# One closing unit for each tile of the shared expert, and the small transfers of the softmax shifts issued by ScalarE

## The chip, the cores and the metric

The kernel runs on one core of a Trainium2 chip. The metric is the time of one execution on the device in microseconds (us), as the median of several runs; less is better. TensorE is called PE here, VectorE DVE, ScalarE ACT, GpSimd POOL and SyncE SP; SP does nothing but issue transfers and wait. A transfer that an engine issues goes into a queue of that engine, and all queues share the core's 16 DMA engines.

## The reference

One post-norm transformer layer over 8 batches of 512 tokens, 256 wide, in float32:

```python
x = layernorm(x + attention(x, w_qkv, w_out))          # 16 heads of 16, causal
x = layernorm(x + ffn(x))
# ffn: softmax router over 16 experts, the 6 highest of probs + gate_b are taken,
#   y = sum over them of prob * (silu(x W1' + b1) * (x W3' + b3)) W2' + b2     (176 hidden)
#   z = (silu(x ws1' + bs1) * (x ws3' + bs3)) ws2' + bs2                       (352 hidden)
#   ffn(x) = y + z
```

## The kernel before

The engines run programs of their own, written out by hand, and meet at semaphores. There are four stages.

**Attention.** A loop over 8 batches `b`, in each four groups `g` of four heads, in each eight substeps `s`; the order of each engine's work in a substep is fixed by tables (`PE_ORDER`, `MISC`, `FILLS_OF_SUB`, `SHIFT_AT`). Group number G is 4b + g. PE computes the scores twice: once two groups ahead to find each row's maximum (line 722 and the causal mask of line 724; DVE reduces them, line 1347), and once transposed (line 737) for the exponential on ACT (line 1059), 12 fills to a group. For the second, the negative maximum is part of the operand: `stack_q` has 96 rows with three bfloat16 parts of q and below them 3 rows, the *shift*, with three bfloat16 parts of the maxima. PE transposes the maxima of the next group (stage `m`, line 769), ACT copies them out, DVE splits them in three (`split_shift`, lines 1405 to 1411), and three transfers of 4 KB each carry them into the rows (`load_shift`, line 537). At the start of a group PE waits for the stack and for the shift:

```python
pe.wait_ge(stack_loaded, 192 * (b + 1))
pe.wait_ge(shift_loaded, 48 * (G + 1))
```

In group 0 of a batch PE also projects q, k and v of the next batch. ACT and POOL split them, and SP issues twelve transfers of 256 KB into the other copy of the stacks (`load_stack`, line 531, six for q and six for k). PE needs all twelve at substep 0 of group 2, where it begins to look for maxima in the next batch's scores. Other stages of the batch before ride along: `t0`, `t1` transpose its attention output (PE line 781, in substep 7 of group 0 and substep 1 of group 1; ACT copies them), `p0`, `p1` project it, `x0`, `x1` transpose the normalized result (group 2), `r`, `d` route and rank. POOL scatters the rows to the experts' regions in DRAM.

In the kernel before SP issues the shift of a group as soon as DVE has split it. In its program it stands between the stack's transfers, the load of the residual and the stores of the normalized rows.

**Shared expert, first part.** 10 of 16 chunks of 256 tokens, three tiles to a chunk, 30 tiles `T`.

**Experts.** 208 blocks of 128 rows; POOL adds each block's result to `x1_d` or `z_d` in DRAM with an accumulating transfer.

**Shared expert, second part, and the closing pass.** Tiles T = 30 to 47. For each tile PE multiplies up (`shared_up`, line 707), ACT applies silu (line 1208), DVE multiplies (`hide`, line 1663), ACT rounds (`high`), `low` takes the remainder (on DVE line 1669, on POOL line 1890), and PE multiplies down (`shared_down`, line 930) two tiles later. The closing pass has 16 units `m` of 256 tokens: SP loads both halves of a unit (`load_final`, line 642), POOL adds them (`final_sum`, line 1927), DVE adds the shared expert's result for the six late chunks and takes mean and variance (`final_stats`, lines 1715 to 1727), POOL raises the variance to the power -0.5 (`final_inverse`, line 1940), DVE forms -mean/std (`final_shift`, line 1733), ACT normalizes (`normalized`, line 1264, two instructions to a unit), SP stores. Before, a unit goes in with every second tile from T = 35 on, so that 7 units have their statistics begun in the tiles and 9 behind them; `low` is DVE's for T below 34 and POOL's from 34 on, and for each unit DVE waits for POOL's inverse straight behind the statistics of the next.

Of the kernel before, what the change touches and what calls it, by code (L numbers as in the profile page):

```python
# [30 lines left out]
GH = 4  # L31
NG = HEADS // GH
SUBS = 8
STACK = 6 * HD
SHIFT_ROWS = 3
# [16 lines left out]
HALF = 2  # L52
# [55 lines left out]

SPLIT_X_AT, LOW_X_AT = (3, 1), (3, 3)
# [49 lines left out]
FINAL_ORDER = (10, 0, 11, 1, 12, 2, 13, 3, 14, 4, 15, 5, 6, 7, 8, 9)  # L159
FINAL_FROM = T1 + 5  # L160
DVE_LOW_AFTER = 4
# [5 lines left out]


def final_of(T):

    return (T - FINAL_FROM) // 2 if T >= FINAL_FROM and (T - FINAL_FROM) % 2 == 0 else None


FINAL_IN_TILES = len([T for T in range(T_SH) if final_of(T) is not None])


# [48 lines left out]
def postln_layer(nc, xT, x, wqk, wv, wo, gw, gb, ws, we, b13, b2s, out):  # L225
# [17 lines left out]
    with ctx:  # L243
# [274 lines left out]
        def _(sp):  # L518
# [14 lines left out]
            def load_shift(G, par, gpar, g):  # L533

                sp.wait_ge(shift_step, 3 * G + 3)
                for j in range(SHIFT_ROWS):
                    sp.dma_start(
                        stack_q[par][STACK + j:STACK + j + 1, GH * g:GH * g + GH, :], shift_parts[gpar][j][:]
                    ).then_inc(shift_loaded, 16)

            def iteration(b, par):
# [8 lines left out]
                load_shift(4 * b + 1, par, 1, 1)  # L550
# [6 lines left out]
                load_shift(4 * b + 2, par, 0, 2)  # L557
# [6 lines left out]
                load_shift(4 * b + 3, par, 1, 3)  # L564
# [5 lines left out]
                if not last:  # L570
                    load_shift(4 * b + 4, 1 - par, 0, 0)
# [94 lines left out]
            load_shift(0, 0, 0, 0)  # L666
# [381 lines left out]
        def _(act):  # L1048
# [211 lines left out]
            def normalized(m):  # L1260
                i = FINAL_ORDER[m]
                act.wait_ge(fin_shift_done, m + 1)
                for q in range(HALF):
                    last = nc.scalar.activation(fin_x[i][:, q, :], fin_x[i][:, q, :], ACT.Identity,
                                                bias=fin_shift[:, i, q:q + 1], scale=fin_rstd[:, i, q:q + 1])
                last.then_inc(fin_done, 1)
# [62 lines left out]
        def _(dve):  # L1329
# [380 lines left out]
            def final_stats(m):  # L1710
# [7 lines left out]
                for q in range(HALF):  # L1718
                    last = nc.vector.bn_stats(fin_stats[:, i, q, :], fin_x[i][:, q, :])
# [3 lines left out]
                for q in range(HALF):  # L1723
                    last = nc.vector.bn_aggr(fin_mv[:, i, q, :], fin_stats[:, i, q, :])
                last.then_inc(fin_mv_done, 1)
                dve.wait_ge(fin_mv_done, m + 1)
                nc.vector.tensor_scalar(fin_var[:, i, :], fin_mv[:, i, :, 1], EPS, None, ALU.add).then_inc(
                    fin_var_done, 1)

            def final_shift(m):  # L1730
                i = FINAL_ORDER[m]
                dve.wait_ge(fin_rstd_done, m + 1)
                nc.vector.scalar_tensor_tensor(fin_shift[:, i, :], fin_mv[:, i, :, 0], -1.0, fin_rstd[:, i, :], ALU.mult,
                                               ALU.mult).then_inc(fin_shift_done, 1)
# [32 lines left out]
            for m in range(FINAL_IN_TILES, HALVES):  # L1767
                final_stats(m)
                final_shift(m - 1)
            final_shift(HALVES - 1)  # L1770


        @block.gpsimd
        def _(pool):
# [162 lines left out]
            def final_inverse(m):  # L1937
                i = FINAL_ORDER[m]
                pool.wait_ge(fin_var_done, m + 1)
                nc.gpsimd.tensor_tensor(fin_rstd[:, i, :], fin_var[:, i, :], half_neg[:, 0:HALF], ALU.pow).then_inc(  # L1940
                    fin_rstd_done, 1)

            for T in range(T1 + DVE_LOW_AFTER, T_SH):
                m = final_of(T)
# [3 lines left out]
                if m:  # L1948
                    final_inverse(m - 1)
                low(T)  # L1950
                if m is not None:
                    final_sum(m + 2)
            for m in range(FINAL_IN_TILES, HALVES):
                final_inverse(m - 1)
                if m + 2 < HALVES:
                    final_sum(m + 2)
            final_inverse(HALVES - 1)
# [66 lines left out]
```

## Time and profile before

| | us |
|---|---|
| median of 3 runs (lowest to highest) | 1195.66 (1192.45 to 1196.21) |
| the profiled execution, its own time | 1196.26 |
| its span from first to last instruction | 1194.3 |
| attention, about 30 to 518 of the span | 488 |
| shared expert, first part, and tables, 518 to 620 | 102 |
| experts, 620 to 1120 | 500 |
| second part and closing pass, 1120 to the end | 74 |

Over the whole span PE is busy for 1059.2 us (89%), DVE 745.7 (62%), ACT 666.2 (56%), POOL 750.0 (63%). The profiled execution took 0.6 us more than the median, 1.96 us of its time lie outside its span. In the rows below a line such as `[2.71 <-DMA stack_q<-shift_l]` says that the engine sat idle for 2.71 us ahead of this instruction and what ended the wait.

### The profile page before, as it was taken

The page shows a single profiled execution, that of the slowest core. Times are in us where ns is not written, and L with a number is a line of the kernel's source. Part 1 is how long each engine was busy: PE and PEld are TensorE (multiplying, and loading weights), DVE is VectorE, ACT ScalarE, POOL GpSimd, SP SyncE. Part 2 cuts the span into 40 slices and gives each one's busy share as a digit, 9 for nine tenths or more (in the row PEclk, how much of TensorE's full clock was granted, in tenths as well). Part 3 has the DMA queues.
Part 4 walks back from the last instruction along what each step waited for, and adds up shares of the span by engine and source line. Part 5 has one row for each costly group of instructions (what it writes and reads, how often), then busy time and mean ns, then how long its engine had stood idle before and what let it go on. Part 6 is the DMA issues. An engine that isn't in the chain of part 4 may idle for free.

```text
span 1194.3 us, 28292 instructions
## 1 busy us (share of the span) xinstructions
PE 1059.2 (89%) x8039; PEld 859.4 (72%) x8040; DVE 745.7 (62%) x2402; ACT 666.2 (56%) x1672; POOL 750.0 (63%) x686
## 2 busy tenths in 40 slices
PE   4979999989999987878869999999999999999780
PEld 3436555555555553458859999999999999999780
DVE  6657777777786777546745555555555555555346
ACT  3357666666665655654535555555555555555344
POOL 3122447877787777856745666666666666666556
PEclk8689998999998999788989999999999999999986
DMA  6351535554545455457985777777777666666772
GB/s 167 99 125 36 126 103 150 166 162 146 169 155 159 150 161 167 153 191 221 323 265 99 118 119 116 118 119 118 117 117 115 117 113 116 117 111 109 172 257 101
DMA packets 125385, 172.01 MB, mean 144 GB/s; under 512 B 17408, under 2 KB 97792, under 8 KB 125312
## 3 DMA queue, kind: packets, MB, share of 16 engines
q1 hardware_dynamic: 77328, 107.23, 32.3%
q0 software_dynamic: 39168, 54.42, 25.1%
q10 hardware_dynamic: 8816, 9.44, 2.5%
q8 instruction: 40, 0.66, 0.2%
q14 instruction: 33, 0.27, 0.1%
HBM read 67.43 MB, written 78.03 MB: 122 GB/s over the span
## 4 chain that ended last, share of the span: by engine, by line
PE 53%; DMA 19%; DVE 11%; POOL 5%; issue 4%; ACT 4%; SPq 4%; ACTq 0%; POOLq 0%; DVEq 0%
DMA z_d<-y_sb,tokens 12%; PE psum L962 11%; PE psum L989 8%; PE psum L707 7%; PE psum L749 5%; PE psum L722 4%; PE psum L737 4%; DVE rowmax L1347 3%; DMA stack_q<-shift_l 3%; PE psum L949 3%; PE psum L973 3%; PE psum L958 2%; SPq L531 2%; PE psum L724 2%; POOL k_l L1799 1%
## 5 line engine op out<-in xcount | busy, mean ns | idle before, releaser
L1347 DVE TENSOR_REDUCE rowmax<-psum 128x1 f32<-128x512 f32 (+3 forms) x352 | 215.8, 635 | 84.3 <-PE psum L724 81.4
L1059 ACT ACTIVATE probs<-psum 128x512 f32<-128x512 f32 (+2 forms) x384 | 183.6, 530 | 142.9 <-PE psum L737 142.7
L1837 POOL DMA_INDIRECT xs_d<-x1p,index x192 | 200.5, 1044 | 47.5 <-issue 44.0
L1916 POOL DMA_INDIRECT x_d<-y_sb,tokens x104 | 162.6, 1564 | 88.6 <-ACT y_sb L1247 54.5
L1916 POOL DMA_INDIRECT z_d<-y_sb,tokens x104 | 162.2, 1559 | 88.6 <-issue 43.0
L1681 DVE TENSOR_TENSOR xb_lo<-psum,xb_hi 128x256 fp32r<-128x256 f32 x208 | 88.4, 425 | 197.7 <-ACT xb_hi L1050 197.7
L962 PE MATMUL psum<-we_hi_lo,xb_hi 128*128 x832 | 202.2, 324 | 0.0
L722 PE MATMUL psum<-stack_k,stack_q 96*128 96x256 bf16 (+3 forms) x512 | 146.3, 323 | 44.8 <-DMA stack_q<-shift_l 19.8
L1247 ACT ACTIVATE y_sb<-psum,combine 128x256 f32<-128x256 f32 x208 | 98.9, 475 | 139.1 <-PE psum L989 78.0
L989 PE MATMUL psum<-we_hi_lo,hb_hi 88*128 x832 | 174.9, 303 | 0.0
L1780 POOL TENSOR_SCALAR_AFFINE_SELECT probs<-probs 128x512 f32<-128x512 f32 x128 | 88.3, 690 | 117.5 <-ACT probs L1059 116.7
L962 PEld LDWEIGHTS psum<-we_hi_lo,xb_hi 128*128 128x128 f32 x832 | 148.5, 190 | 0.0
L962 PE MATMUL psum<-we_hi_lo,xb_lo 128*128 x416 | 135.5, 326 | 0.0
L737 PE MATMUL psum<-stack_q,stack_k 99*128 99x256 bf16 (+3 forms) x512 | 123.0, 321 | 4.5 <-issue 1.8
L989 PEld LDWEIGHTS psum<-we_hi_lo,hb_hi 88*128 88x128 f32 x832 | 126.2, 189 | 0.0
L722 PEld LDWEIGHTS psum<-stack_k,stack_q 96*128 96x128 bf16 x512 | 51.3, 101 | 101.4 <-issue 35.2
L989 PE MATMUL psum<-we_hi_lo,hb_lo 88*128 x416 | 116.7, 281 | 0.0
L749 PE MATMUL psum<-probs,values 128*32 128x512 f32 (+3 forms) x1024 | 98.5, 469 | 12.7 <-DVE attn L1424 7.0
L724 PE MATMUL psum<-causal,ident_bf 128*128 128x128 bf16 x512 | 104.9, 231 | 0.0
L1237 ACT ACTIVATE hb<-psum 128x176 f32<-128x176 f32 x208 | 66.1, 318 | 66.4 <-PE psum L962 65.0
L1686 DVE TENSOR_TENSOR hb_lo<-psum,hb_hi 88x256 fp32r<-88x256 f32 x208 | 87.1, 419 | 3.5 <-ACT hb_hi L1050 3.2
L949 PE MATMUL psum<-ident,xb 128*128 128x128 f32 x416 | 80.1, 275 | 5.5 <-DVE we_hi_lo L1339 5.5
(197 smaller groups left out, 2298.0 us busy)
## 6 DMA issues: line engine op xcount, KB each, us to landing
xb<-xs_d SPq DMA_DIRECT2D x208, 138.0 KB
w_raw<-in_we SPq DMA_DIRECT2D x16, 608.0 KB, 4.2
stack_q<-q_h SPq DMA_DIRECT2D x24, 256.0 KB
stack_k<-k_h SPq DMA_DIRECT2D x24, 256.0 KB
x1T<-x1T_d ACTq DMA_DIRECT2D x10, 512.0 KB, 7.9
xT_raw<-in_xT SPq DMA_DIRECT2D x9, 512.0 KB
stack_q<-q_m SPq DMA_DIRECT2D x16, 256.0 KB
stack_k<-k_m SPq DMA_DIRECT2D x16, 256.0 KB
```

Of the source, the lines that this page charges most:

```text
L722: nc.tensor.matmul(dst, stack_q[par][0:STACK, head, qt * P:qt * P + P], stack_k[par][0:STACK, head, 0:width], start=True, stop=False)
L724: last = nc.tensor.matmul(dst[:, width - P:width], ident_bf[:], causal[:], start=False, stop=True)
L737: last = nc.tensor.matmul(st[f % ST_BANKS][:, i * width:(i + 1) * width], stack_k[par][0:STACK + SHIFT_ROWS, head, kt * P:kt * P + P], sta ...
L749: last = nc.tensor.matmul(ov[32 * j:32 * j + 32, kt * P:S], values[par][:, kt, GH * g + j, :], probs[kt][:, j, :], start=kt == 0, stop=kt ...
L949: last = nc.tensor.transpose(xt_ps[k % 2][:, d * P:d * P + P], xb[k % 4][:, d * P:d * P + P], ident[:])
L962: last = nc.tensor.matmul(uv, (xb_hi, xb_lo)[a][k % 2][:, d, :], w_flat[:, bass.ds(at + b * W_COLS + d * UP, UP)], start=False, stop=d == ...
L989: last = nc.tensor.matmul(y, (hb_hi, hb_lo)[a][k % 2][0:rows, d, :], w_flat[0:rows, bass.ds(at + b * W_COLS + W2_AT + d * D, D)], start=d ...
L1059: nc.scalar.activation(probs[kt][:, heads[0]:heads[0] + n, :], st[f % ST_BANKS][:, 0:n * width].rearrange("p (h t) -> p h t", h=n), ACT.Ex ...
L1247: nc.scalar.activation(y_sb[k % 4][:], y_ps[k % 2][:, 0:D], ACT.Copy, scale=combine[:, k:k + 1]).then_inc(y_out, 1)
L1347: nc.vector.reduce_max(rowmax[gpar][:, heads[0]:heads[0] + n, qt], src, AX.X).then_inc(sm_free, 1)
L1837: nc.gpsimd.indirect_dma_start(out=xs_d[:, :], out_offset=bass.IndirectOffsetOnAxis(ap=index[tp][:, n:n + 1], axis=0), in_=x1p[tp][:, n // ...
L1916: nc.gpsimd.indirect_dma_start(out=(x1_d, z_d)[k % 2][:, :], out_offset=bass.IndirectOffsetOnAxis(ap=tokens[:, k:k + 1], axis=0), in_=y_sb ...
```

## The change

In attention three transfers of each shift are no longer in SP's program (but for the very first group's) and are issued by ACT into ACT's queue, at fixed places of its program: the shift of group 1 in substep 7 of group 0, that of group 2 in substep 6 of group 1, that of group 3 in substep 5 of group 2, and that of the next batch's group 0 in substep 5 of group 3. In such a substep they stand behind ACT's copies of the substep's stage. In the closing pass a unit goes in with every tile from T = 36 on, 12 in the tiles and 4 behind them; units are taken in another order; DVE keeps `low` up to T = 35; variance, inverse and shift are done for two units at a time; ACT normalizes a unit four tiles after its statistics.

```diff
+LOAD_SHIFT_AT = {(0, 7): 1, (1, 6): 2, (2, 5): 3, (3, 5): 4}
-FINAL_ORDER = (10, 0, 11, 1, 12, 2, 13, 3, 14, 4, 15, 5, 6, 7, 8, 9)
-FINAL_FROM = T1 + 5
-DVE_LOW_AFTER = 4
+FINAL_ORDER = (10, 0, 1, 11, 2, 3, 12, 4, 5, 13, 6, 7, 14, 8, 9, 15)
+FINAL_FROM = DVE_LOW_UP_TO = T1 + 6
...
 # SP, one batch
-                load_shift(4 * b + 1, par, 1, 1)
...
-                load_shift(4 * b + 2, par, 0, 2)
...
-                load_shift(4 * b + 3, par, 1, 3)
...
-                if not last:
-                    load_shift(4 * b + 4, 1 - par, 0, 0)
...
 # ACT
+            def load_shift(G, par, gpar, g):
+
+                act.wait_ge(shift_step, 3 * G + 3)
+                for j in range(SHIFT_ROWS):
+                    act.dma_start(
+                        stack_q[par][STACK + j:STACK + j + 1, GH * g:GH * g + GH, :], shift_parts[gpar][j][:]
+                    ).then_inc(shift_loaded, 16)
...
                             middle_part(b + 1, PARTS_AT[g, s])
                         if (g, s) == SOFTMAX_AT and not (whole and b == 0):
                             router_softmax(b - 1)
+                        if (g, s) in LOAD_SHIFT_AT and has(b, g, "m"):
+                            n = LOAD_SHIFT_AT[g, s]
+                            load_shift(4 * b + n, par if n < NG else 1 - par, n % 2, n % NG)
...
-                m = final_of(T)
-                if m:
-                    normalized(m - 1)
+                if T >= FINAL_FROM + 4:
+                    normalized(T - FINAL_FROM - 4)
             high(T_SH - 1)
-            for m in range(FINAL_IN_TILES, HALVES + 1):
-                normalized(m - 1)
+            for m in range(T_SH - FINAL_FROM - 4, HALVES):
+                normalized(m)
...
 # DVE
-            for T in range(T1 + 2, T_SH):
-                hide(T)
-                if T - 1 < T1 + DVE_LOW_AFTER:
+            for T in range(T1 + 2, FINAL_FROM + HALVES):
+                if T < T_SH:
+                    hide(T)
+                if T - 1 < DVE_LOW_UP_TO:
                     low(T - 1)
-                m = final_of(T)
-                if m is not None:
+                m = T - FINAL_FROM
+                if m >= 3 and m % 2:
+                    final_shift((m - 3) // 2)
+                if m >= 0:
                     final_stats(m)
-                    if m:
-                        final_shift(m - 1)
...
 # POOL
+            for T in range(DVE_LOW_UP_TO, FINAL_FROM + HALVES):
+                m = T - FINAL_FROM
+                if T < T_SH:
+                    low(T)
                 if m == 0:
                     final_sum(0)
                     final_sum(1)
...
+                if m >= 2 and m % 2 == 0:
+                    final_inverse((m - 2) // 2)
                 if m + 2 < HALVES:
                     final_sum(m + 2)
-            final_inverse(HALVES - 1)
+            final_inverse(HALVES // 2 - 1)
```

## Rows read from the trace of the kernel before

**Rows 1.** Windows by stage: busy time of each engine, granted clock, DMA share, GB/s.

```profile
30.00:518.00 488.00, 438.54 (x3500) 257.91 (x3504) 350.74 (x856) 294.12 (x658) 310.20 (x339) 0.92 0.48 142
...
1120.00:1195.00 75.00, 33.87 (x251) 32.27 (x249) 34.96 (x117) 27.96 (x61) 42.46 (x48) 0.78 0.58 186
```

**Rows 2.** Waits in attention: total us, times, longest.

```profile
PE psum L722 <- DMA stack_q<-shift_l: 19.8, 8, 5.5
```

**Rows 3.** Timeline of PE, batch 3, end of group 0 and start of group 1.

```profile
235.63 0.66 PE L781 MATMUL psum<-ident,attn 128*128 128x128 f32 x4
236.12 0.38 PE L722 MATMUL psum<-stack_k,stack_q 96*128 96x512 bf16 x1
```

**Rows 4.** Timeline of ACT, batch 3, at the four places of the change but the last.

```profile
236.32 0.60 ACT L1050 ACTIVATE t_hi<-psum 128x512 fp32r<-128x512 f32 x1 [0.86 <-PE psum L781]
...
237.29 0.63 ACT L1050 ACTIVATE k_m<-rest 128x512 bf16<-128x512 f32 x1
...
247.28 1.15 ACT L1059 ACTIVATE probs<-psum 128x512 f32<-128x512 f32 x3 [3.23 <-PE psum L737]
...
262.38 0.64 ACT L1050 ACTIVATE t_raw<-psum 128x512 f32<-128x512 f32 x1
```

**Rows 5.** Timeline of PE, batch 3, start of groups 2 and 3.

```profile
248.20 1.07 PE L749 MATMUL psum<-probs,values 128*32 128x512 f32 x8
251.98 0.38 PE L722 MATMUL psum<-stack_k,stack_q 96*128 96x512 bf16 x1 [2.71 <-DMA stack_q<-shift_l]
...
264.50 0.59 PE L737 MATMUL psum<-stack_q,stack_k 99*128 99x512 bf16 x2 [0.87 <-issue]
```

**Rows 6.** Timeline of SP, batch 3: the last shift transfer of groups 1 and 2.

```profile
231.61 0.59 SPq L537 DMA_DIRECT2D stack_q<-shift_l  x1
...
247.69 0.60 SPq L537 DMA_DIRECT2D stack_q<-shift_l  x1
```

**Rows 7.** The chain that ended last: start, us (issue to landing).

```profile
44.55 2.62 DMA stack_q<-shift_l
...
247.69 4.20 DMA stack_q<-shift_l
```

**Rows 8.** Timeline of ACT's issues, one of three in a row.

```profile
563.48 0.52 ACTq L1284 DMA_DIRECT2D x1T_d<-t_hi  x1
```

**Rows 9.** Timeline of PE: first fill of groups 2 and 3, batches 1 and 2.

```profile
135.62 0.59 PE L737 MATMUL psum<-stack_q,stack_k 99*128 99x512 bf16 x2
...
145.70 0.61 PE L737 MATMUL psum<-stack_q,stack_k 99*128 99x512 bf16 x2
...
192.66 1.06 PE L737 MATMUL psum<-stack_q,stack_k 99*128 99x512 bf16 x2
...
205.13 0.61 PE L737 MATMUL psum<-stack_q,stack_k 99*128 99x512 bf16 x2
```

**Rows 10.** Timeline of PE, second part: the long wait.

```profile
1135.59 0.80 PE L930 MATMUL psum<-ws_hi_lo,h_hi 128*128 128x256 f32 x2 [7.79 <-POOL h_lo L1890]
```

**Rows 11.** Timeline of POOL, second part: the second unit's sum.

```profile
1133.59 1.26 POOL L1927 TENSOR_TENSOR fin_x<-fin_x,fin_z 128x512 f32<-128x512 f32 x1 [1.85 <-DMA fin_z<-z_d]
```

**Rows 12.** Groups by shape, 1120 us to the end: busy, mean ns, idle before.

```profile
L1927 POOL TENSOR_TENSOR fin_x<-fin_x,fin_z 128x512 f32<-128x512 f32 x16 | 20.4, 1272 | 7.0 <-DMA fin_z<-z_d 7.0
...
L1719 DVE BATCH_NORM_STATS2 fin_stats<-fin_x 128x6 f32<-128x256 f32 x32 | 11.9, 414 | 0.2
L1940 POOL TENSOR_TENSOR fin_rstd<-fin_var,half_neg 128x2 f32<-128x2 f32 x16 | 11.3, 703 | 1.9 <-DVE fin_var L1727 1.4
...
L1890 POOL TENSOR_TENSOR h_lo<-hidden,h_hi 128x256 fp32r<-128x256 f32 x14 | 10.2, 730 | 14.5 <-ACT h_hi L1050 14.5
```

**Rows 13.** Groups by shape, whole span: a power of four values to a partition.

```profile
L1810 POOL TENSOR_TENSOR rstd<-var_eps,half_neg 128x4 f32<-128x4 f32 x8 | 8.4, 1054 | 0.7
```

**Rows 14.** Timeline of ACT: the last two units.

```profile
1188.12 2.07 ACT L1264 ACTIVATE fin_x<-fin_x,fin_shift,fin_rstd 128x256 f32<-128x256 f32 x4 [0.23 <-DVE fin_shift L1733]
```

**Rows 15.** Timeline of DVE: one of the slow small operations.

```profile
1184.49 0.89 DVE L1727 TENSOR_SCALAR fin_var<-fin_mv 128x2 f32<-128x2 f32 x1
```

More of the change, by code:

```diff
@@ L166 @@
 GAP, GAP2 = 352, 3160
-def final_of(T):
-    return (T - FINAL_FROM) // 2 if T >= FINAL_FROM and (T - FINAL_FROM) % 2 == 0 else None
-FINAL_IN_TILES = len([T for T in range(T_SH) if final_of(T) is not None])
 def fills_of(g, s):
@@ L531, in load_stack, with load_first_shift @@
                         sp.dma_start(dst[j:STACK:STACK // HD, :, :], parts[n][part][:]).then_inc(stack_loaded, 16)
-            def load_shift(G, par, gpar, g):
-                sp.wait_ge(shift_step, 3 * G + 3)
+            def load_first_shift():
+                sp.wait_ge(shift_step, 3)
                 for j in range(SHIFT_ROWS):
-                    sp.dma_start(
-                        stack_q[par][STACK + j:STACK + j + 1, GH * g:GH * g + GH, :], shift_parts[gpar][j][:]
-                    ).then_inc(shift_loaded, 16)
+                    sp.dma_start(stack_q[0][STACK + j:STACK + j + 1, 0:GH, :], shift_parts[0][j][:]).then_inc(
+                        shift_loaded, 16)
             def iteration(b, par):
@@ L665, in _ @@
             sp.dma_start(xT_raw[:], xT[1]).then_inc(xT_loaded, 16)
-            load_shift(0, 0, 0, 0)
+            load_first_shift()
             sp.wait_ge(small_loaded, 32)
@@ L1261, in normalized @@
                 i = FINAL_ORDER[m]
-                act.wait_ge(fin_shift_done, m + 1)
+                act.wait_ge(fin_shift_done, m // 2 + 1)
                 for q in range(HALF):
                     last = nc.scalar.activation(fin_x[i][:, q, :], fin_x[i][:, q, :], ACT.Identity,
-                                                bias=fin_shift[:, i, q:q + 1], scale=fin_rstd[:, i, q:q + 1])
+                                                bias=fin_shift[:, m, q:q + 1], scale=fin_rstd[:, m, q:q + 1])
                 last.then_inc(fin_done, 1)
@@ L1718, in final_stats @@
                 for q in range(HALF):
-                    last = nc.vector.bn_stats(fin_stats[:, i, q, :], fin_x[i][:, q, :])
+                    last = nc.vector.bn_stats(fin_stats[:, m, q, :], fin_x[i][:, q, :])
                 last.then_inc(fin_stats_done, 1)
@@ L1723, in final_stats, with final_shift @@
                 for q in range(HALF):
-                    last = nc.vector.bn_aggr(fin_mv[:, i, q, :], fin_stats[:, i, q, :])
+                    last = nc.vector.bn_aggr(fin_mv[:, m, q, :], fin_stats[:, m, q, :])
                 last.then_inc(fin_mv_done, 1)
[L1726 to L1734, printed above, removed]
+                if m % 2:
+                    two = slice(m - 1, m + 1)
+                    dve.wait_ge(fin_mv_done, m + 1)
+                    nc.vector.tensor_scalar(fin_var[:, two, :], fin_mv[:, two, :, 1], EPS, None, ALU.add).then_inc(
+                        fin_var_done, 1)
+            def final_shift(k):
+                two = slice(2 * k, 2 * k + 2)
+                dve.wait_ge(fin_rstd_done, k + 1)
+                nc.vector.scalar_tensor_tensor(fin_shift[:, two, :], fin_mv[:, two, :, 0], -1.0, fin_rstd[:, two, :],
+                                               ALU.mult, ALU.mult).then_inc(fin_shift_done, 1)
             for T in range(T1):
@@ L1757, in _ @@
             low(T1)
-            for T in range(T1 + 2, T_SH):
-                hide(T)
-                if T - 1 < T1 + DVE_LOW_AFTER:
+            for T in range(T1 + 2, FINAL_FROM + HALVES):
+                if T < T_SH:
+                    hide(T)
+                if T - 1 < DVE_LOW_UP_TO:
                     low(T - 1)
-                m = final_of(T)
-                if m is not None:
+                m = T - FINAL_FROM
+                if m >= 3 and m % 2:
+                    final_shift((m - 3) // 2)
+                if m >= 0:
                     final_stats(m)
-                    if m:
-                        final_shift(m - 1)
[L1767 to L1770, printed above, removed]
+            final_shift(HALVES // 2 - 1)
         @block.gpsimd
@@ L1936, in _, with final_inverse @@
             by_blocks(pool, blocks)
[L1937 to L1940, printed above, removed]
+            def final_inverse(k):
+                two = slice(2 * k, 2 * k + 2)
+                pool.wait_ge(fin_var_done, k + 1)
+                nc.gpsimd.tensor_tensor(fin_rstd[:, two, :], fin_var[:, two, :],
+                                        half_neg[:].rearrange("p (m q) -> p m q", q=HALF), ALU.pow).then_inc(
                     fin_rstd_done, 1)
-            for T in range(T1 + DVE_LOW_AFTER, T_SH):
-                m = final_of(T)
+            for T in range(DVE_LOW_UP_TO, FINAL_FROM + HALVES):
+                m = T - FINAL_FROM
+                if T < T_SH:
+                    low(T)
                 if m == 0:
@@ L1947, in _ @@
                     final_sum(1)
[L1948 to L1954, printed above, removed]
+                if m >= 2 and m % 2 == 0:
+                    final_inverse((m - 2) // 2)
                 if m + 2 < HALVES:
                     final_sum(m + 2)
-            final_inverse(HALVES - 1)
+            final_inverse(HALVES // 2 - 1)
 def laid_out(i):
```

## The prediction

> **What bounds the kernel now.** I read the windows by stage first. In attention PE is busy for 439 of 488 us, and in the second part and closing pass for 34 of 75 us [rows 1]. So in attention whatever holds PE up is paid almost in full; in the closing pass it is not PE that sets the time. In the experts' stage, between them, nothing is edited.
>
> Next the waits of attention. PE waited for the shift 8 times, 19.8 us in all, once 5.5 us [rows 2]: that is the start of group 2, once to a batch, and one wait at the very first group. Without the longest, 14.3 us are left for seven waits, about 2.3 us for each of six batches and little for the seventh. In batch 3 it is 2.71 us, from 249.27 to 251.98 [rows 5]. There the shift's last transfer was issued at 247.69, behind the six transfers of k's stack in the same queue, and took 4.20 us to land [rows 6, 7]. The idle 0.87 us at the start of group 3 [rows 5] is of the same kind though it is called "issue"; it is the longest such wait in the six middle batches, and three of them have none. At the start of group 1 PE goes from `t0`'s transposes at 235.63 straight into the next group at 236.12: no wait [rows 3], since SP had issued the shift by 231.61 [rows 6].
>
> **The change in attention.** SP's issue is tied to DVE alone, ACT's is tied to all that stands ahead of it in ACT's program. So for each place I ask when ACT gets there and when PE needs the shift. One transfer's issue on ACT takes 0.52 us and about 0.04 to the next [rows 8], so the third begins about 1.15 us after the first. For landing the trace has 2.62 us (first group, little beside it) and 4.20 us (behind the stack) [rows 7]. I take 3.0, nearer to the first since ACT's queue is otherwise empty there, but the 16 engines are not; 2.6 and 4.2 are the bounds.
>
> *Group 1 (substep 7 of group 0).* In this substep ACT first copies the output of `t0`. Those transposes are the last thing PE does before group 1, so ACT can't be early: `t_hi` starts at 236.32, then `t_raw`, then the middle part of k at 237.29 [rows 4], and only then the three issues. The third begins at about 237.35 + 1.15 = 238.5 and lands at 241.5. PE is ready at 236.1 [rows 3]. A stall of 5.4 us is new (5.0 to 6.6). It is a matter of order, not of load: the program makes PE wait for something that ACT may only begin once PE has got there.
>
> *Group 2 (substep 6 of group 1).* ACT gets there with fill 10, the second of the three that start at 247.28 [rows 4], so at about 247.8; third issue 248.95, landed 251.95. PE is ready at 249.27 [rows 5]: 2.7 us, where 2.3 is the mean of before. So +0.4 (0 to 1.6). What was meant to go, the queueing behind k's stack, is gone, but the issue is later by as much. k's stack itself is no longer a bound, as PE comes 5.4 us later to this point.
>
> *Group 3 (substep 5 of group 2).* Here ACT's copies of `x1` stand ahead; `t_raw` starts at 262.38 [rows 4], third issue 263.6, landed 266.6, against 264.50 before [rows 5]: +2.1 here, about +2.8 in the batches without a wait before. I take 2.5 (2.1 to 3.7).
>
> *Group 0 of the next batch (substep 5 of group 3).* No copies stand ahead, and PE needs it some three substeps later; I cost it at nothing. If it came 2 us later than I think, 1 us a batch would be added.
>
> *ACT's own time.* Twelve issues to a batch are 12 x 0.56 = 6.7 us. They lie in the stalls that they cause, and ACT is idle for 194 of 488 us [rows 1]; nothing more.
>
> *PE's clock.* From batch 1's first fill of group 2 to that of group 3 PE took 145.70 - 135.62 = 10.1 us, after a wait of about 2 us and with matmuls at full speed (0.59 us for two). In batch 2 it took 205.13 - 192.66 = 12.5 us; there the wait was followed by matmuls at 1.06 us for the same two, the lower of the two levels (1.2 instead of 2.4 GHz) [rows 9]. So a stall may be followed by some us at half speed, worth up to 2.4 us. Two more stalls to a batch: 0 to 4 us, and I take 2.0, as DVE bounds part of group 3.
>
> Sum for batches 1 to 6: 5.4 + 0.4 + 2.5 + 2.0 = 10.3 us each, 62 in all. Batch 0 has no `t0` and no `x1`, and its group 2 waited 5.5 us before, which takes up group 1's delay: +2. Batch 7 has `t0` but little to hide behind: +5. Attention: +69 us (lower bounds 47, upper 106).
>
> The Trainium skill (DMA: Bandwidth & Descriptors, "Anatomy of one DMA") puts a transfer's fixed cost at about 2.0 us. No row shows a landing of a shift as short; by it each stall would be 1.0 us shorter than I take, some 18 us over six batches, an estimate from that page. Its table of advice there has it that one should issue early and wait late, which the first place does the reverse of.
>
> **The change in the closing pass.** Before, PE's longest wait is 7.79 us [rows 10]: `low` of T = 35 stood on POOL behind two sums that waited for the loads until 1133.59 [rows 11]. Now DVE does `low` up to 35, POOL's `low` of 36 stands ahead of the sums, and that of 37 is the first behind them. POOL runs the second sum to 1134.85 and the third to about 1136.4. From there on POOL is the engine with most work: for a tile 0.70 (`low`) + 1.25 (sum) + half of a power on four values, 1.05 [rows 12, 13], together 2.5 us, where PE needs about 2.2. Until its last sum and the inverse behind it POOL has 11 lows, 13 sums and 7 inverses: 7.7 + 16.3 + 7.2 = 31.2 us, to 1167.6. Then the last pair: DVE adds (0.7), takes the statistics (two of 0.41 and what follows, 1.2) [rows 12] and the variance (0.2), POOL inverts (1.0), DVE shifts (0.1), ACT normalizes two units in 2.07 [rows 14]: 5.3 us, to 1172.9. Before, ACT ended at 1190.19 [rows 14]. The same bookkeeping for the kernel before ends 3.3 us ahead of its trace, since small DVE operations take up to 0.89 us beside POOL's [rows 15]; half of that I give back. So the end comes at 1174.5, and the change is worth -15.7 us there (-11 with all of it and the loads in the way, -18 with nothing). The 4 us of storing behind the last unit stay.
>
> **Rivals.**
> *A. The shift is in time anyway, and the kernel gets faster.* That needs ACT's issues at group 1 and 3 to be off PE's path, all 5.4 us of the first: ACT would have to reach them before PE's last stage. Then attention would lose the 2.3 us waits or keep them, and the time would be 1196 - 16 - (0 to 14), 1166 to 1180. Against it stands the order in [rows 3, 4]. It turns at 16 us: attention must cost under 2 us a batch. 4%.
> *B. Faster landing, no clock loss, part of the stalls taken up by waits for DVE that follow.* Lower bounds: 1196.3 + 47 - 18 = 1225, and 1205 to 1225 if DVE's waits take up half. 14%.
> *C. Landing at 4.2 us each time (the q stack is still moving at group 1) and clock loss at each stall.* 1196.3 + 106 - 11 = 1291; halfway there, 1270 and more. 13%.
> *D. The closing pass gives nothing, as the loads or the stores bound it.* 1196.3 + 69 = 1265. 4%.
> The Trainium skill (DMA: Bandwidth & Descriptors, "Issuing engines are not separate DMA queues") says that a second engine's queue saves only the issuing time, as all run on the same 16 engines. Were even the order behind the stack kept so, group 2 would lose 1.2 us more a batch, 7 us in all; that lies within C.
>
> **How the numbers follow.** My forecast: 1196.3 + 69 - 15.7 = 1249.6 of the profiled execution's own time, which lies 0.6 above the median; so 1249, and I round towards the lower bounds to 1248. It holds 65%. The range of 8 in 10 reaches into B and C: 1220 to 1277. A measurement here tells about 0.3% (3.6 us) from no change. Faster 4%, same 2%, slower 94%.
>
> **What would show it.** In the trace after: PE waits for the shift about 5 us at every group 1 from batch 1 on, with ACT's issues behind the middle part of k; 2 to 3 us at groups 2 and 3; none at group 0; a batch of about 69 us instead of 59; more slices with half the clock. In the closing pass PE without the 7.8 us wait at T = 35 and one at about T = 36 or 37 in its place, POOL without gaps from there on, four units behind the last tile. I am wrong if PE enters group 1 without a wait, or if the time from the last expert block to the end has not shrunk by 10 us or more.

## The result, and the profile after

| | before | after |
|---|---|---|
| median, us | 1194.66 | 1232.51 |
| lowest to highest of 4 runs | 1192.45 to 1196.21 | 1228.41 to 1242.45 |
| span of the profiled execution | 1194.3 | 1228.4 |
| start of POOL's last accumulating transfer (expert blocks done) | 1122.99 | 1171.15 |
| from there to the end of ACT's last normalization | 67.2 | 54.1 |

The median before is that of four runs here, one more than above. The change makes the kernel slower: ratio 1.033, 95% interval 1.026 to 1.040. The two parts go in opposite directions, as forecast. What lies ahead of the closing pass grew by 48.2 us, the closing pass shrank by 13.2, and the stores behind it by another 0.9; together +34.1, the difference of the spans.

The waits of the changed kernel first (total us, times, longest). The first row is PE at the start of group 1 in batches 0 to 6, the second at the start of groups 2 and 0, the third mostly at the start of group 3; they answer to [rows 2], where 19.8 us were all there was for the shift but for 1.8 us of "issue" at group 3. (The one wait for k's first stack ahead of the loop, 11.4 us, is in both kernels.)

```profile
PE psum L707 <- DMA stack_q<-q_l: 39.8, 7, 6.1
...
PE psum L707 <- DMA stack_q<-shift_l: 12.8, 11, 3.0
PE psum L722 <- issue: 10.5, 8, 2.2
```

One group 1, batch 3, in the timeline of all engines (start, us, what, and in brackets the idle time ahead of it). It answers to [rows 3, 4, 6], where PE went on without a wait.

```profile
253.96 0.66 PE L766 MATMUL psum<-ident,attn 128*128 128x128 f32 x4
254.65 0.60 ACT L1035 ACTIVATE t_hi<-psum 128x512 fp32r<-128x512 f32 x1 [0.86 <-PE psum L766]
254.66 0.51 ACTq L1140 DMA_DIRECT2D stack_q<-shift_h  x1
254.69 1.13 SPq L523 DMA_DIRECT2D stack_q<-q_l  x1
255.14 0.59 ACT L1035 ACTIVATE t_raw<-psum 128x512 f32<-128x512 f32 x1
255.20 1.59 ACTq L1140 DMA_DIRECT2D stack_q<-shift_m  x1
255.62 0.63 ACT L1035 ACTIVATE k_m<-rest 128x512 bf16<-128x512 f32 x1
...
256.83 0.73 ACTq L1140 DMA_DIRECT2D stack_q<-shift_l  x1
260.34 0.58 PE L707 MATMUL psum<-stack_k,stack_q 96*128 96x512 bf16 x1 [5.73 <-DMA stack_q<-q_l]
...
260.83 1.06 PE L722 MATMUL psum<-stack_q,stack_k 99*128 99x512 bf16 x2
```

PE is ready at 260.34 - 5.73 = 254.61. ACT begins to issue with `t_hi`, its first copy of PE's last stage, and the third issue starts 2.2 us after PE was ready. PE goes on 3.5 us later. Behind the stall two fills take 1.06 us: PE runs at the lower of its two levels (1.2 GHz; granted clock 0.50 from 261 to 265). The profile names `q_l` as what ended the wait, though this group needs nothing of the next batch's stack. That name was the first hint of a second cause. The windows of these microseconds show it (busy time of PE, PEld, DVE, ACT, POOL, then granted clock, DMA share, GB/s):

```profile
252.00:254.00 2.00, 2.00 (x25) 1.03 (x22) 2.00 (x4) 1.64 (x4) 1.47 (x3) 1.00 0.92 246
254.00:256.00 2.00, 0.61 (x8) 0.37 (x4) 0.55 (x1) 1.35 (x3) 1.23 (x2) 1.00 1.04 269
256.00:258.00 2.00, 0.00 (x0) 0.00 (x0) 0.00 (x0) 0.25 (x1) 2.00 (x2) 1.00 1.02 278
258.00:260.00 2.00, 0.00 (x0) 0.00 (x0) 0.00 (x0) 0.00 (x0) 0.19 (x1) 0.85 0.48 110
```

The 16 DMA engines are full from 252 on, with q's stack above all (SP's queue takes 80% of their time from 252 to 259, POOL's scatters 16%), and the shift is there a good microsecond after they run empty, at about 259.

Batch 7 has no next batch, and so no q's stack. It shows the order alone:

```profile
519.62 0.60 ACT L1035 ACTIVATE t_hi<-psum 128x512 fp32r<-128x512 f32 x1 [2.87 <-PE psum L766]
519.62 0.51 ACTq L1140 DMA_DIRECT2D stack_q<-shift_h  x1
520.17 0.61 ACTq L1140 DMA_DIRECT2D stack_q<-shift_m  x1
520.81 0.61 ACTq L1140 DMA_DIRECT2D stack_q<-shift_l  x1
...
522.66 0.59 PE L707 MATMUL psum<-stack_k,stack_q 96*128 96x512 bf16 x1 [3.08 <-issue]
```

The DMA share is 0.02 here, no issue takes over 0.61 us, PE goes on 1.85 us after the third issue's start, and the stall is 3.08 us instead of 5.7. Batch 0 is the other half: it has no `t0`, and stalls 5.28 us all the same.

The stall has a tail. ACT's second `k_m` stands behind fills that PE can't start, so k's stack is late as well: before it began at 241.02, 4.9 us after PE was ready for group 1 [rows 3]; now it begins 9.75 us after that point:

```profile
262.47 0.63 ACT L1035 ACTIVATE k_m<-rest 128x512 bf16<-128x512 f32 x1
263.18 1.15 POOL L1794 TENSOR_TENSOR k_l<-rest,k_m 128x512 bf16<-128x512 f32 x1 [4.99 <-ACT k_m L1035]
...
264.36 0.55 SPq L523 DMA_DIRECT2D stack_k<-k_h  x1
...
274.75 0.61 ACTq L1140 DMA_DIRECT2D stack_q<-shift_l  x1
276.62 0.38 PE L707 MATMUL psum<-stack_k,stack_q 96*128 96x512 bf16 x1 [1.17 <-DMA stack_q<-shift_l]
```

At group 2 (the last two lines, which answer to [rows 5, 6]) the wait is now 1.17 us instead of 2.71. The DMA engines were empty by then (share 0.06 from 274 to 276), and with empty engines PE went on 1.87 us after the last issue's start. PE's first fill of group 0 shows what each batch pays in all: it starts at 47.58, 108.32, 172.49, 237.07, 307.85, 371.67, 439.12 and 503.85, and the growth against before, batch by batch, is 5.8, 7.6, 5.3, 10.9, 5.5, 7.3 and 5.6 us, and 4.9 in the last batch up to its group 3. Of these 53 us about 4.5 are given back in the stages that follow.

The closing pass: PE's longest wait, which answers to [rows 10], then two tiles of POOL and DVE in the steady part, then ACT's last units, which answer to [rows 14].

```profile
1180.71 0.52 PE L915 MATMUL psum<-ws_hi_lo,h_hi 128*128 128x256 f32 x2 [4.32 <-DVE fin_x L1710]
...
1195.93 1.28 POOL L1922 TENSOR_TENSOR fin_x<-fin_x,fin_z 128x512 f32<-128x512 f32 x1
1196.39 0.85 DVE L1724 TENSOR_SCALAR fin_var<-fin_mv 128x4 f32<-128x4 f32 x1
1197.15 0.47 DVE L1658 SCALAR_TENSOR_TENSOR hidden<-psum,bias,hidden 128x256 f32<-128x256 f32 x1
...
1197.66 0.42 ACT L1035 ACTIVATE h_hi<-hidden 128x256 fp32r<-128x256 f32 x1 [0.87 <-DVE hidden L1658]
...
1198.15 0.74 POOL L1885 TENSOR_TENSOR h_lo<-hidden,h_hi 128x256 fp32r<-128x256 f32 x1 [0.94 <-ACT h_hi L1035]
1198.85 1.01 POOL L1936 TENSOR_TENSOR fin_rstd<-fin_var,half_neg 128x4 f32<-128x4 f32 x1
1199.85 1.28 POOL L1922 TENSOR_TENSOR fin_x<-fin_x,fin_z 128x512 f32<-128x512 f32 x1
1199.90 1.25 DVE L1730 SCALAR_TENSOR_TENSOR fin_shift<-fin_mv,fin_rstd 128x4 f32<-128x4 f32 x1
...
1223.13 2.07 ACT L1260 ACTIVATE fin_x<-fin_x,fin_shift,fin_rstd 128x256 f32<-128x256 f32 x4 [1.21 <-DVE fin_shift L1730]
```

The 7.79 us wait is down to 4.32. From then on POOL is the busiest engine, but not without gaps: in every second tile it waits 0.94 to 1.12 us for ACT's `h_hi`. Two tiles take 5.86 us (`low` at 1198.15 and again at 1204.01), 2.93 us for one.

### The profile page after: what moved, and what is told of

It is laid out like the page before. It is cut to its first block, busy times and chain, and to the rows that moved or that the text cites. A ratio compares the mean times of both kernels' runs of the same rounds, so it can differ in the third digit from the quotient of the medians.

```text
span 1228.4 us, 28268 instructions
## 1 busy us (share of the span) xinstructions
PE 1066.3 (87%) x8039; PEld 859.4 (70%) x8040; DVE 743.4 (61%) x2388; ACT 668.1 (54%) x1672; POOL 744.2 (61%) x676
## 4 chain that ended last, share of the span: by engine, by line
PE 48%; DMA 24%; DVE 11%; issue 6%; ACT 4%; POOL 3%; SPq 2%; ACTq 1%; POOLq 0%; DVEq 0%
DMA z_d<-y_sb,tokens 16%; PE psum L947 9%; PE psum L692 7%; PE psum L974 6%; PE psum L722 5%; PE psum L707 5%; PE psum L734 4%; DVE rowmax L1342 3%; DMA stack_q<-q_l 3%; DMA stack_q<-shift_l 2%; SPq L523 2%; PE psum L934 2%; PE psum L958 2%; PE psum L943 2%; PE psum L709 1%
## 5 line engine op out<-in xcount | busy, mean ns | idle before, releaser
L707 PE MATMUL psum<-stack_k,stack_q 96*128 96x256 bf16 (+3 forms) x512 | 149.3, 329 | 78.7 <-DMA stack_q<-q_l 39.8
L734 PE MATMUL psum<-probs,values 128*32 128x512 f32 (+3 forms) x1024 | 102.5, 485 | 14.3 <-POOL probs L1775 7.5
L722 PEld LDWEIGHTS psum<-stack_q,stack_k 99*128 99x128 bf16 x512 | 41.3, 102 | 64.0 <-issue 37.3
```

What stands on the lines that cost most here:

```text
L707: nc.tensor.matmul(dst, stack_q[par][0:STACK, head, qt * P:qt * P + P], stack_k[par][0:STACK, head, 0:width], start=True, stop=False)
L722: last = nc.tensor.matmul(st[f % ST_BANKS][:, i * width:(i + 1) * width], stack_k[par][0:STACK + SHIFT_ROWS, head, kt * P:kt * P + P], sta ...
L734: last = nc.tensor.matmul(ov[32 * j:32 * j + 32, kt * P:S], values[par][:, kt, GH * g + j, :], probs[kt][:, j, :], start=kt == 0, stop=kt ...
```

## The experiments

Each experiment is the changed kernel with the edit shown. "Waits" are those of PE at the start of groups. Ratios are to the kernel before, run on the same chip beside it. That kernel took 1197.09 us beside the first four, 1198.11 beside the next four, 1236.45 (another chip) beside the next three and 1194.05 beside the last, so ratios are compared, not times.

**1 and 2. Either part alone.** First the closing pass alone, with all shifts back in SP's program as before; then the shifts on ACT alone, with the closing pass of before.

```diff
-LOAD_SHIFT_AT = {(0, 7): 1, (1, 6): 2, (2, 5): 3, (3, 5): 4}
+LOAD_SHIFT_AT = {}
...
+                load_shift(4 * b + 1, par, 1, 1)
+                load_shift(4 * b + 2, par, 0, 2)
+                load_shift(4 * b + 3, par, 1, 3)
+                if not last:
+                    load_shift(4 * b + 4, 1 - par, 0, 0)
```

> The closing pass as changed, all shifts issued by SyncE as in the kernel before. If the two halves of the change are independent, attention is as before and the closing pass is worth what the trace after shows between the last accumulating transfer and ScalarE's end: 54.1 us instead of 67.2, so about 13 us less than before, 1181 to 1182. Rival: part of that gain came only from a different start of the pass, then less than 10 us.

> The shifts issued by ScalarE as changed, the closing pass as before. My theory puts the whole loss here: 1194.7 + 48 = about 1243, and the sum of this and the other half reproduces the changed kernel within 4 us. A rival in which the two interact would leave a gap of more than 5 us.

Measured: the closing pass alone 1180.93 us, ratio 0.984 (0.976 to 0.991); the shifts alone 1252.3 us, ratio 1.037 (1.027 to 1.048), with 40.0 us of waits at group 1 over 7. So the closing pass is a gain and the shifts are the whole loss. The two changes of time, -16.2 and +55.2 us, add up to +39.0, where both together cost 37.9: neither needs the other. The shifts alone took 9 us more than I expected.

**3 and 4. Which shift costs.** In one, SP issues group 1's shift as before and ACT the others; in the other ACT issues group 1's alone.

```diff
-LOAD_SHIFT_AT = {(0, 7): 1, (1, 6): 2, (2, 5): 3, (3, 5): 4}
+LOAD_SHIFT_AT = {(1, 6): 2, (2, 5): 3, (3, 5): 4}      # the first
+LOAD_SHIFT_AT = {(0, 7): 1}                            # the second
```

> The changed kernel with the shift of group 1 alone given back to SyncE. Theory of order: the 5.7 us stall at each group 1 goes, and with it the slow clock behind it and the delay of k's stack; group 2 and 3 cost what they cost in the trace after, about 1 us less and 1 us more than before. So 1181 to 1190. Rival theory of the queue (each shift on ScalarE's queue costs about the same, as it lands late beside other transfers): a third of the 48 us goes, about 1217.

> Only the shift of group 1 is issued by ScalarE, the rest by SyncE, closing pass as changed. Theory of order: nearly the whole loss is here, 1225 to 1235. Theory of the queue: 1181 + 16 = about 1197.

Measured: without group 1 on ACT 1195.92 us, ratio 0.998 (0.995 to 1.002); with group 1 alone on ACT 1222.2 us, ratio 1.021 (1.013 to 1.029). Against the closing pass alone, beside which both ran, group 1 costs 41 us and the other three together 15, more than the 0 to 9 that I expected of them. With only group 1 on ACT its waits are 40.6 us over 7, and the wait at group 2 is nearly gone (1.8 us in batch 0, next to none behind it), though SP issues that shift and in its old place. With group 1 on SP the wait at group 2 is what it was, 2.2 to 3.1 us in the middle batches. So moving that shift to another queue doesn't take the 2.3 us at group 2 away.

**5 and 6. An earlier place, and one ahead of the copies.** The first moves group 1's issue one substep earlier; the second keeps the substeps and puts the issues ahead of the stage's copies in ACT's program.

```diff
-LOAD_SHIFT_AT = {(0, 7): 1, (1, 6): 2, (2, 5): 3, (3, 5): 4}
+LOAD_SHIFT_AT = {(0, 6): 1, (1, 6): 2, (2, 5): 3, (3, 5): 4}      # the first
```

```diff
 # the second: ahead of the copies, not behind them
+                        if (g, s) in LOAD_SHIFT_AT and has(b, g, "m"):
+                            n = LOAD_SHIFT_AT[g, s]
+                            load_shift(4 * b + n, par if n < NG else 1 - par, n % 2, n % NG)
                         stage = MISC.get((g, s))
```

> The changed kernel with the shift of group 1 issued one substep earlier, in substep 6 of group 0, behind the copies of k there. By the trace after, the issues begin at about 252.5 instead of 254.7 there and the third lands 3.5 us behind its start, so the stall at group 1 shrinks from 5.7 to about 3 us: 1232 - 7 x 3 = about 1211. Rival theory, that the transfers land when the stack of q has drained whatever the time of their issue: the stall stays near 5 us and the time near 1230.

> The changed kernel with each shift's issue ahead of ScalarE's copies of the same substep instead of behind them. Theory of order: at group 1 the issues no longer wait for the last transposes, and begin about 1.3 us earlier; the stall shrinks to 4.4 us, that of group 3 goes from about 1 us to 0.3. About 1232 - 7 x 1.7 = 1220. If the drain of q's stack decides: 1228 to 1232.

Measured: one substep earlier 1230.19 us, ratio 1.023 (1.017 to 1.030), and the stalls at group 1 are still 35.0 us over 7, 5.0 each. Ahead of the copies 1223.97 us, ratio 1.018 (1.009 to 1.026), with 38.0 us over 7 at group 1 and 6.8 over 6 mostly at group 3. Here my theory of the first fell: ACT's order alone doesn't make the stall. Batch 3 of the first, ACT's engine and its queue:

```profile
253.40 0.51 ACTq L1140 DMA_DIRECT2D stack_q<-shift_h  x1
...
253.94 1.55 ACTq L1140 DMA_DIRECT2D stack_q<-shift_m  x1
...
255.52 1.47 ACTq L1140 DMA_DIRECT2D stack_q<-shift_l  x1
257.08 0.38 ACT L1044 ACTIVATE probs<-psum 128x256 f32<-128x256 f32 x1 [2.44 <-issue]
```

and its windows:

```profile
254.00:256.00 2.00, 1.74 (x15) 0.57 (x12) 1.68 (x3) 0.64 (x2) 0.73 (x1) 1.00 0.96 267
256.00:258.00 2.00, 0.00 (x0) 0.00 (x0) 0.00 (x0) 0.92 (x3) 0.36 (x1) 1.00 1.05 248
258.00:260.00 2.00, 0.00 (x0) 0.00 (x0) 0.00 (x0) 0.96 (x2) 1.74 (x3) 1.00 0.95 250
260.00:262.00 2.00, 1.32 (x4) 0.54 (x5) 0.60 (x1) 0.17 (x1) 0.90 (x1) 0.57 0.08 29
```

The issues begin 2.4 us ahead of the moment at which PE is ready (253.40 against 260.68 - 4.93 = 255.75), where in the changed kernel they begin with it. But two of them last 1.5 us, ACT stands still for 2.44 us behind them, and PE goes on at 260.68, when the DMA engines have just run empty. The shift's packets are in another queue than q's stack and still come through only with its end. Batch 7, without that stack, has no stall at group 1 in either of these runs.

**7. All four early.** Group 1 in substep 5 of group 0, the others one substep earlier, all ahead of the copies; the issue of group 1 is then ahead of q's stack.

```diff
-LOAD_SHIFT_AT = {(0, 7): 1, (1, 6): 2, (2, 5): 3, (3, 5): 4}
+LOAD_SHIFT_AT = {(0, 5): 1, (1, 5): 2, (2, 4): 3, (3, 4): 4}
```

> The changed kernel with all four shifts issued by ScalarE as soon as VectorE's split allows it: substeps 5, 5, 4 and 4, ahead of the copies. Theory of order: no stall at group 1 and 3; group 2 keeps a wait of at most what it was. 1178 to 1184, as with SyncE. Theory of the queue or of ScalarE's time (12 issues of 0.6 us to a batch delay its exponentials): 1190 to 1200.

Measured: 1198.77 us, ratio 1.001 (0.999 to 1.004). Batch 3, the queues of ACT and SP:

```profile
233.68 0.61 ACTq L1140 DMA_DIRECT2D stack_q<-shift_l  x1
234.23 1.85 SPq L523 DMA_DIRECT2D stack_q<-q_h  x3
```

The last issue starts half a microsecond ahead of the stack's first and takes 0.61 us again. There is no stall at group 1 (0.38 us in batch 0 is all). At group 2 the waits are as before. So the stall went as the theory of order has it, but the time is that of its rival; more on that under 12.

**8. Group 2 alone.** ACT issues only the shift of group 2, one substep earlier than in the change; SP has the others.

```diff
-LOAD_SHIFT_AT = {(0, 7): 1, (1, 6): 2, (2, 5): 3, (3, 5): 4}
+LOAD_SHIFT_AT = {(1, 5): 2}
```

> Only the shift of group 2 is issued by ScalarE, in substep 5 of group 1, the rest by SyncE, closing pass as changed. If the wait at group 2 is the shift's queueing behind k's stack, it goes from 2.3 to under 1 us: 1181 - 7 x 1.5 = about 1171. If k's stack itself lands hardly earlier than the shift, nothing is gained: 1179 to 1183.

Measured: 1185.14 us, ratio 0.989 (0.982 to 0.995), and 22.3 us of waits at group 2 over 7, beside 20.1 over 7 with the closing pass alone. Out of the queue behind k's stack the shift still lands slowly: in the middle batches PE goes on 2.6 to 4.0 us after the third issue's start, where it takes 1.9 us with empty engines. The engines are full with k's stack beyond the moment at which PE is ready (in batch 3 the share is 1.04 up to 250 and 0.80 from 250 to 252; PE is ready at 250.50). But the run isn't clean. ACT's third issue starts only 0.2 to 0.8 us ahead of PE's being ready, SP's started 1.1 to 2.5 us ahead before, so the shift also came about 1 us later. What an issue from another queue at the old moment would give is not shown; nor is how much of this wait would be left for k's stack itself, which PE needs at the same place.

**9 and 10. q's stack held back until the shift has landed.** This takes away the load on the DMA engines and leaves ACT's order. In 9 ACT's places are those of the change, in 10 group 1's is one substep earlier, as in 5.

```diff
                     if not first:
                         sp.wait_ge(st_full, SF * NG * b)
+                    sp.wait_ge(shift_loaded, 48 * (4 * b + 2))
                     load_stack(b + 1, 1 - par)
```

> The changed kernel, but SP begins the six transfers of q's stack (and k's behind them) only when the shift of group 1 has landed. ACT's places stay as changed. THEORY (the stall at group 1 is half ACT's order and half q's stack: the shift's packets are done only when the stack's are): ACT's three issues begin with t_hi and take 0.55 us each again, the last lands some 2 us later in empty engines, and the stall at group 1 falls from 5.7 to 3 to 3.8 us; 7 x 2.3 = 16 us less, 1216 us, if the stack's later start costs nothing at group 2; up to 3 us a batch of it may come back there. RIVAL (the stall is ACT's order alone): stalls of 5 us or more stay, and the time stays at 1232 or rises.

> As the run before, and ACT issues the shift of group 1 one substep earlier (substep 6 of group 0). With q's stack in the way that place brought the stall only from 5.7 to 5.0 us. THEORY: both causes are gone, so the shift lands 1 to 1.5 us after PE is ready or earlier; stalls at group 1 of 0 to 1.5 us, 7 x 4.5 = 31 us less than the changed kernel, about 1200 us. RIVAL (something else at group 1 holds PE, such as the buffers of psum or DVE): a stall of 3 us or more, 1215 us and above.

Measured: 9 took 1290.23 us, ratio 1.045 (1.039 to 1.052), 10 took 1266.24 us, ratio 1.024 (1.018 to 1.031). Neither time is what I expected, but both stalls at group 1 are. Batch 3 of 9:

```profile
262.44 0.61 ACTq L1141 DMA_DIRECT2D stack_q<-shift_l  x1
...
264.29 0.38 PE L708 MATMUL psum<-stack_k,stack_q 96*128 96x512 bf16 x1 [3.07 <-issue]
```

With nearly empty DMA engines (share 0.04 from 262 to 264) PE goes on 1.85 us after the last issue's start, and the stall is 3.1 us (1.8 in batch 0, 3.1 in all others); in 10 it is 0.7 to 1.4 us. So with q's stack out of the way ACT's order makes 3.1 us, as in batch 7 of the changed kernel, and the stack makes them 5.7. The two don't simply add up, and both must go for the stall to go: the place alone took 0.7, the stack alone 2.6, both together 4.7 or so. The times went wrong at group 2. With q's stack late, k's runs straight behind it and the DMA share stays over 1.0 from 266 to 280:

```profile
278.00:280.00 2.00, 0.57 (x8) 0.00 (x0) 1.82 (x6) 0.38 (x1) 1.74 (x3) 1.00 1.02 307
280.00:282.00 2.00, 0.00 (x0) 0.00 (x0) 0.00 (x0) 0.00 (x0) 1.81 (x3) 1.00 0.43 150
```

and behind batch 0 PE waits 2.9 to 5.4 us at group 2 in 9, and 4.8 to 6.1 in 10, where the changed kernel has 1.2. I had allowed for at most 3 us of this.

**11. The closing pass with POOL's inverse first.** All shifts on SP, as in 1, and in every second tile the inverse stands ahead of `low`.

```diff
+                if m >= 2 and m % 2 == 0:
+                    final_inverse((m - 2) // 2)
                 if T < T_SH:
                     low(T)
...
-                if m >= 2 and m % 2 == 0:
-                    final_inverse((m - 2) // 2)
```

> The closing pass of the change alone (all shifts on SP), with one swap: in every second tile POOL does the inverse of two units ahead of its low, not behind it. In the closing pass alone POOL waits 0.94 us for ACT's h_hi in each second tile, straight ahead of low and inverse. THEORY (that gap is a matter of POOL's order: the inverse fits into it, and DVE gets it earlier): five gaps of 0.94 us go, 4 to 5 us less than the closing pass alone, 1176 us. RIVAL (a ring POOL, DVE, ACT sets the pace: DVE's shift follows the inverse, hide stands behind it, h_hi behind that, low behind that): h_hi comes no earlier against low, PE gets h_lo later, and the time stays within 2 us of 1181.

Measured: ratio 0.985 (0.980 to 0.990), by time not to be told from run 1. POOL in the steady part:

```profile
1184.13 0.76 POOL L1898 TENSOR_TENSOR h_lo<-hidden,h_hi 128x256 fp32r<-128x256 f32 x1
1184.83 1.32 POOL L1935 TENSOR_TENSOR fin_x<-fin_x,fin_z 128x512 f32<-128x512 f32 x1
1186.08 1.04 POOL L1949 TENSOR_TENSOR fin_rstd<-fin_var,half_neg 128x4 f32<-128x4 f32 x1
1187.07 0.75 POOL L1898 TENSOR_TENSOR h_lo<-hidden,h_hi 128x256 fp32r<-128x256 f32 x1
1187.76 1.31 POOL L1935 TENSOR_TENSOR fin_x<-fin_x,fin_z 128x512 f32<-128x512 f32 x1
1189.00 0.76 POOL L1898 TENSOR_TENSOR h_lo<-hidden,h_hi 128x256 fp32r<-128x256 f32 x1
```

All gaps for `h_hi` but one are gone: two tiles take 4.87 us (1184.13 to 1189.00) instead of 5.86, 2.44 us for one. From the start of the third sum to the end of the last inverse it is 36.3 us (1172.39 to 1208.72), against 40.2 in run 1 (1140.03 to 1180.25). In the trace the theory holds, 3.9 us; no ring of waits sets the pace. In that execution the third sum came 0.6 us later behind the last accumulating transfer than in run 1 (12.0 us against 11.3), which leaves 3.3 us, less than the interval of the ratio (6 us to either side) can tell.

**12. Group 1 alone on ACT, early.**

```diff
-LOAD_SHIFT_AT = {(0, 7): 1, (1, 6): 2, (2, 5): 3, (3, 5): 4}
+LOAD_SHIFT_AT = {(0, 5): 1}
```

and ahead of the copies.

> The new closing pass, and of the shifts ACT issues only that of group 1, in substep 5 of group 0 ahead of the copies, that is before q's stack is in the queues; SP issues the others as before. All four placed early on ACT gave a ratio of 1.001, the closing pass alone 0.984. THEORY (place, not engine, decides at group 1: issued before q's stack, the shift is landed long before PE needs it, and the other 1.7% belong to the shifts of groups 2, 3 and 0): no stall at group 1, ratio 0.98 to 0.99. RIVAL (three issues on ACT in substep 5 cost by themselves, as ACT's exponentials there come later): no stall at group 1 either, but a ratio of 0.995 or more.

Measured: 1181.44 us, ratio 0.989 (0.986 to 0.993). No stall at group 1; 19.3 us over 7 at group 2, as before. So ACT may issue this shift at little or no cost if it does so in time. There was nothing to gain at group 1, where PE didn't wait before. The four versions with ratios under 0.99 (1, 8, 11, 12) have no stall at group 1, and SP issues their shifts of groups 3 and 0. Between 7 and 12 lies 1.2%, which the runs explain only in part. In the profiled executions (spans 1185.1 and 1172.0) PE waits for the shift at groups 3 and 0 for 6.8 us in 7 and 1.7 us in 12, and from its first fill to that of group 3 in the last batch it takes 458.7 us in 7 and 453.6 in 12. The other 8 us lie behind that, where the two programs are the same, and most timed executions of 7 took some 12 us more than its profiled one; that stays open.

## Why the prediction was right, and where its sum was off

The time came out at 1232.5 where I had 1248, within the range, and the cause is the one that I forecast. The sum was 15 us too large. By its steps:

*Group 1, +5.4 us.* Measured 5.3 to 6.1, mean 5.7. The size is right and its account half right. I had ACT's issues behind `t_hi`, `t_raw` and `k_m`; they began with `t_hi`, 1.2 us sooner. And I had 1.15 us from the first issue to the third and 3.0 us for landing, where it took 2.2 and 3.5, since q's stack still filled the engines. These errors, -1.2, +1.0 and +0.5, cancel but for 0.3 us: that the size fits is luck. "It is a matter of order, not of load" is half wrong. Batch 7 and runs 5, 9 and 10 show that the order I named makes 3.1 us by itself and that q's stack, which I had kept as a bound only (rival C), makes them 5.7. I had also looked for this wait from batch 1 on; batch 0, without `t0`, has 5.3 us of it.

*Group 2, +0.4 us.* Measured -1.1 (1.2 us instead of 2.3). The landing of 3.0 us was too long for empty engines: 1.87. The sentence "what was meant to go, the queueing behind k's stack, is gone" names the wrong thing. In runs 3, 7 and 8 ACT issues this shift, and the wait stays at 1.8 to 3.3 us: the load of k's stack on the DMA engines holds the shift up in another queue too. The stall at group 1 gave them the time to run empty; in run 4 that alone takes the wait away, with the shift in SP's queue. "k's stack itself is no longer a bound" holds for the changed kernel, but only thanks to that stall, and runs 9 and 10 show it come back.

*Group 3, +2.5 us.* Measured 0.4 to 2.2 us of waits, 1.3 in the mean, against 0 to 0.87, so about +1. ACT's issues again didn't wait until the copies had run, and in batch 3 the landing took 2.6 us.

*Group 0, 0.* Right but for batch 0, with 1.6 us.

*Clock, +2.0 us.* The middle batches grew by 42.3 us, 7.0 each instead of 10.3; less 5.7 - 1.1 + 1.0 = 5.6 us of stalls, 1.4 us are left for half clock and what follows a stall. Nearly all of it lies in two batches: group 3 took 18.96 us in batch 3, at a mean granted clock of 0.73, and 15.90 in batch 5, at 0.89, behind waits of 1.84 and 2.19 us; in the other four, behind waits of 1.05 to 1.15 us, it took 13.6 to 13.9 us at 1.00.

*Batch 0, +2 us; batch 7, +5 us.* Measured +5.8 and +4.9. In batch 0 I had group 2's old wait of 5.5 us take up the stall; it fell only to 3.0, as k's stack is late with it. Further 4.5 us were given back behind attention, which I had not foreseen. Attention in all: 48, where the lower bound was 47 and the sum 69. Of the 21 us between 69 and 48, group 2 and group 3 are 9 each. (The bounds aren't quite what their terms give: (5.0 + 0 + 2.1 + 0) x 6 + 7 = 50 and (6.6 + 1.6 + 3.7 + 4) x 6 + 7 = 102, not 47 and 106.)

*Closing pass, -15.7 us.* Measured -14.1 in the trace, stores included, and -16 by the times of run 1. POOL took 2.93 us for a tile, not 2.5; run 11 shows that 2.44 is there to be had if `low` needn't wait. PE's long wait went to 4.3 us; it didn't vanish.

Of the rivals, A (in time anyway) is out by the stalls. B names what happened to the sum, a shorter landing and little loss to the clock, and its 1205 to 1225 lies just below the time measured. C's landing behind q's stack is real, but it is 3.5 us at group 1, not 4.2, and at group 2 1.9. D is out by run 1. Of the signs I had named, the wait at group 1, the gain of over 10 us behind the experts and PE's shorter wait in the closing pass came true; the 2 to 3 us at groups 2 and 3 (1.2 and 1.4), a batch of 69 us (65.9) and POOL without gaps didn't.

The Trainium skill (DMA: Bandwidth & Descriptors, "Anatomy of one DMA") puts the fixed part of a transfer at about 2.0 us, in a section on transfers that GpSimd issues; those here are ACT's. I had set it aside because no row showed it. The traces come near it where the engines are empty (1.85 and 1.87 us from the issue's start to PE's), and it would have brought the sum nearer; at group 1, with the engines full, it took 3.5 us. Its section "Issuing engines are not separate DMA queues" says that transfers of all engines run on the same 16 and interleave; runs 5 and 8 agree, and run 5 is sharper: small packets in ACT's queue came through only at the end of SP's.

## What to carry to other kernels

Before a small transfer is moved to another engine's queue, look at two things at the moment of its issue: what stands ahead of it in the new engine's program, above all work that waits for the very engine that needs the transfer, and whether the 16 DMA engines are full. In these runs another queue helped with neither; an issue ahead of the large transfers did, at group 1. And a wait that a profile puts down to a queue is tested by taking the small transfer out of it alone before anything is built on it, with the issue at its old moment, which run 8 missed by about 1 us. Look too for a batch or a block of the trace that lacks one of two suspected causes: batch 7 separates them without a run.

## What the runs showed of the hardware

ACT's DMA issues overtook its own arithmetic: the first issue began at 254.66, together with `t_hi`, while `t_raw` (255.14) and `k_m` (255.62), which stand ahead of it in the program, had not begun. In batch 7 it is the same (519.62 both). What held the issue back was, by these rows, the wait for PE that `t_hi` has ahead of it.

An issue can cost more when the DMA engines are full: up to 1.47 to 1.59 us instead of 0.51 to 0.61 in the batches shown, and the engine behind it stands still (2.44 us on ACT in run 5). Not every one does: the first of the three took 0.51 us at a share of 1.0 too.

In the closing pass DVE's tiny operations end with POOL's large ones: `fin_shift` (1199.90, 1.25 us, four values to a partition) beside the sum (1199.85, 1.28 us), and `fin_var` (to 1197.24) with the sum before it (to 1197.21). Where POOL is idle, as at 1222.94 and 1221.65, they take 0.16 and 0.17 us. The Trainium skill (SBUF — State Buffer, "Who interferes with whom") has VectorE and GpSimd share one port pair under an exclusive lock for a whole instruction; for `fin_shift`, with two inputs in SBUF, the trace agrees. `fin_var` has one such input and was held up as well; what that section says of operations with one input hangs on a mode that no run here shows.
